# A graph-convolution lookup: ranks that count down, scans beside the roots, and the embedding product scaled one batch later

## The reference, cut to what matters

```python
def gcn_conv(x, W, b, row, col, num_nodes):
    h = x @ W
    loop = jnp.arange(num_nodes)
    row_sl = jnp.concatenate([row, loop]); col_sl = jnp.concatenate([col, loop])
    deg = jax.ops.segment_sum(jnp.ones_like(col_sl, dtype=h.dtype), col_sl, num_segments=num_nodes)
    dinv = jax.lax.rsqrt(jnp.maximum(deg, 1.0))
    norm = dinv[row_sl] * dinv[col_sl]
    return jax.ops.segment_sum(h[row_sl] * norm[:, None], col_sl, num_segments=num_nodes) + b

h1 = gcn_conv(emb, W1, b1, row, col, 25000)      # emb is 25000 x 64, W1 is 64 x 128
lookup = gcn_conv(h1, W2, b2, row, col, 25000)   # W2 is 128 x 64
return lookup[input]                             # 512 x 200 rows of 64
```

## Time and profile before

| | before |
|---|---|
| median of 3 runs | 6868.01 us |
| the profiled execution: its own time | 6869.0 us |
| the profiled execution: span of the profile | 6867.3 us |
| PE busy / DVE busy / ACT busy / POOL busy | 5034.4 / 4014.0 / 2327.5 / 4539.2 us |
| first gather, last gather of round 2, last lookup gather (start) | 786.6, 5835.4, 6857.8 us |
| mean granted TensorE clock | 0.672 |

### The profile page before, as it was taken

How to read it: one execution, slowest core, us unless ns; L and a number is a source line. 1 busy time by engine, 2 the same in 40 slices (tenths; PEclk the granted TensorE clock), 3 DMA queues, 4 the chain that set the end, 5 groups by cost and what they waited for, 6 DMA issues and landing times.

```text
span 6867.3 us, 134775 instructions
## 1 busy us (share of the span) xinstructions
PE 5034.4 (73%) x27534; PEld 4382.0 (64%) x27535; DVE 4014.0 (58%) x13643; ACT 2327.5 (34%) x6633; POOL 4539.2 (66%) x4736
## 2 busy tenths in 40 slices
PE   6868898998999999888788888888888888000000
PEld 5634476776776777888788888888888888000000
DVE  8977798788788798566566555555555555000000
ACT  7957798688688688211000000000000011000000
POOL 0000377777777777777677777777777777677777
PEclk9989999899899899555555555555555555555555
DMA  0001111111111111111111111111111111111111
GB/s 14 0 17 40 28 24 25 26 25 25 26 25 25 27 25 25 30 39 39 33 26 26 26 26 26 26 26 26 27 26 26 35 39 39 44 53 53 53 53 52
DMA packets 184478, 210.98 MB, mean 31 GB/s; under 512 B 81356, under 2 KB 100182, under 8 KB 184336
## 3 DMA queue, kind: packets, MB, share of 16 engines
q0 software_dynamic: 151040, 154.97, 11.4%
q1 hardware_dynamic: 15280, 35.45, 1.4%
q10 hardware_dynamic: 18016, 19.05, 1.0%
HBM read 163.62 MB, written 45.54 MB: 30 GB/s over the span
## 4 chain that ended last, share of the span: by engine, by line
PE 36%; POOL 30%; issue 17%; DVE 7%; DMA 7%; DVEq 2%; ACT 0%; POOLq 0%; SPq 0%; ACTq 0%
PE ps L667 25%; POOL scratch L381 19%; POOL acc L414 11%; PE ps L571 10%; DMA scratch<-table,source 7%; DVE hi_onehot L840 2%; DVE acc L1046 1%; DVE place_i L1001 1%; DVE late L1025 1%; PE ps L720 1%; DVE late L1036 1%; DVE scratch L840 0%; DVEq L1044 0%; DVEq L854 0%; DVE prt_onehot L840 0%
## 5 line engine op out<-in xcount | busy, mean ns | idle before, releaser
L381 POOL DMA_INDIRECT scratch<-table,source x3920 | 3780.5, 964 | 2051.2 <-issue 1104.7
L667 PEld LDWEIGHTS ps<-scratch,late 128*128 128x128 f32 x19520 | 3751.6, 286 | 822.4 <-issue 657.5
L667 PE MATMUL ps<-scratch,late 128*128 x19520 | 3738.9, 369 | 574.5 <-SPq L340 341.7
L1046 DVE TENSOR_TENSOR acc<-acc,ps 128x128 f32 x4880 | 1358.2, 278 | 1378.6 <-PE ps L667 1345.0
L1036 DVE TENSOR_SCALAR late<-ramp,target 128x256 f32<-128x256 f16 x4148 | 1564.2, 377 | 149.0 <-issue 71.5
L467 ACT ACTIVATE late<-prt_onehot,scratch 125x128 f16<-125x128 f16 x4000 | 1236.4, 387 | 306.3 <-DVE prt_onehot L840 151.2
L571 PE MATMUL ps<-late 125*128 125x488 f16 x4000 | 1128.3, 375 | 35.8 <-DVE late L1025 32.9
L414 POOL DMA_INDIRECT acc<-lookup,scratch x800 | 755.1, 944 | 267.4 <-issue 243.4
L543 ACT ACTIVATE acc<-acc,dinv (+1 forms) x196 | 57.5, 340 | 2441.5 <-DVE acc L1046 2441.5
L1025 DVE TENSOR_SCALAR late<-ramp,tcol 125x488 f16<-125x488 f16 x2000 | 697.6, 358 | 48.9 <-PE ps L571 48.3
L571 PEld LDWEIGHTS ps<-late 125*128 125x128 f16 x4000 | 397.6, 119 | 146.2 <-DVE late L1025 60.8
(11 more groups left out here) (149 smaller groups left out, 1106.6 us busy)
## 6 DMA issues: line engine op xcount, KB each, us to landing
scratch<-table,source POOLq DMA_INDIRECT x3920, 2.5
out<-acc SPq DMA_DIRECT2D x40, 640.0 KB, 3.0
acc<-lookup,scratch POOLq DMA_INDIRECT x800, 2.4
table<-acc SPq DMA_DIRECT2D x49, 128.0 KB, 2.5
table<-acc ACTq DMA_DIRECT2D x49, 128.0 KB
lookup<-acc ACTq DMA_DIRECT2D x49, 128.0 KB
late<-embT ACTq DMA_DIRECT2D x47, 128.0 KB, 2.7
scratch<-edge_index SPq DMA_DIRECT2D x2, 976.6 KB
```

The source lines that it names most:

```text
L381: pool.indirect_dma_start(out=place, out_offset=None, in_=table[r], in_offset=bass.IndirectOffsetOnAxis(ap=source[:, t:t + 1], axis=0)).th ...
L667: last = pe.matmul(visit_ps[odd * W8 + k][:, n * FEAT:(n + 1) * FEAT], target_onehot[:, odd * W8 + k, n * P:(n + 1) * P], row, start=True, ...
L1046: dve.tensor_tensor(dst, dst, visit_ps[odd * W8 + k].rearrange("p (n f) -> p n f", f=FEAT), ALU.add).then_inc(visits_added, 1)
```

## The change

There are six edits.

- **Ranks count down.** The three triangles hold -1 in place of 1 (three more memsets on GpSimd). A slot's ranks start at its end and fall. The running sum of the counts, which ends each slot, is used as it comes out of the scan, so that the reduction per block and the subtraction of the counts are gone. Whether a block is empty is now found by comparing neighbouring block ends.
- **Seeds are shifted as they are copied.** The shift of each block's seeds to its first tile was one operation over all 3920 seeds. Now a small array `shift` (5 x 98) is made, and each `seed_ranks` applies it while it writes to PSUM.
- **Scans run beside the roots.** The five scans over the slots stand right after `deg`, each waiting only for its own chunk's counts, ahead of the wait for the square root.
- **The embedding product is scaled a batch later.** VectorE scales the product of batch s-1 in batch s, right behind the block one-hots.
- **Its matmuls are spread.** The eight passes of L720 stand in pairs between the column placements 2 to 5.
- **SyncE loads `embT`.** The load leaves ScalarE's queue and stands in `write_first`, ahead of the wait for the scaled group.

Besides, `w1_sb`, `w2_sb` and `b1_rep` share memory with a one-hot buffer that is idle at the start.

The diff, cut to its core:

```diff
@@ SyncE
                 for s in range(GROUPS):
+                    if s + 2 < GROUPS:
+                        sp.wait_ge(emb_multiplied, s + 1)
+                        sp.dma_start(emb_sb[:, s % 2, :], embT[:, (s + 2) * EN:(s + 3) * EN]).then_inc(emb_loaded[s % 2], 16)
                     sp.wait_ge(emb_scaled, s + 3)
                     sp.dma_start(table_v[0][:, s * ET:(s + 1) * ET, :], acc[:, s * ET:(s + 1) * ET, :]).then_inc(first_written, 16)
@@ GpSimd
+            for triangle in (before, after, itself):
+                pool.memset(triangle[:, :], -1.0).then_inc(ints_made, 1)
+            pool.wait_ge(ints_made, 10)
-            pool.affine_select(out=before[:, :], in_=ones[:, :], compare_op=ALU.is_gt, fill=0.0,
+            pool.affine_select(out=before[:, :], in_=before[:, :], compare_op=ALU.is_gt, fill=0.0,
...
@@ ScalarE, sort_batch
                 for j in range(W8):
                     scale_column(s, j, b)
-                    if load and j == W8 - 2:
-                        act.wait_ge(emb_multiplied, s + 1)
-                        act.dma_start(emb_sb[:, b, :], embT[:, bass.ds((s + 2) * EN, EN)]).then_inc(emb_loaded[b], 16)
@@ TensorE, sort_batch
                 rank_rest(s + 1)
-                pe.wait_ge(emb_loaded[b], i * 16 + 16)
-                pe.wait_ge(emb_scaled, s + 1)
-                for k in range(ET):
+                for j in range(2, W8):
+                    place_column(s, j)
+                    if j >= 2 + ET:
+                        continue
+                    if j == 2:
+                        pe.wait_ge(emb_loaded[b], i * 16 + 16)
+                        pe.wait_ge(emb_scaled, s + 1)
+                    k = j - 2
                     last = pe.matmul(emb_ps[b][:, k * FEAT:(k + 1) * FEAT], emb_sb[:, b, k * P:(k + 1) * P], w12[:, :],
                                      start=True, stop=True)
-                last.then_inc(emb_multiplied, 1)
-                for j in range(2, W8):
-                    place_column(s, j)
+                    if k == ET - 1:
+                        last.then_inc(emb_multiplied, 1)
@@ VectorE, from the degrees on
             dve.wait_ge(turned_degrees, 1)
-            step(dve.tensor_scalar(deg..., 1.0, 1.0, ALU.add, ALU.max))
+            root(dve.tensor_scalar(deg..., 1.0, 1.0, ALU.add, ALU.max))
+            step = chain(base_step)
+            dve.wait_ge(ramps_cast, 2)
+            for c in range(CHUNKS):
+                dve.wait_ge(counts_summed, c + 1)
+                step(dve.tensor_tensor_scan(seed[:, c, :], counts[:, c * SLOTS:(c + 1) * SLOTS], zeros_f[:, 0:SLOTS],
+                                            0.0, ALU.add, ALU.add))
             dve.wait_ge(root_taken, 1)
...
-            step(dve.tensor_reduce(flat, per_slot, AX.X, ALU.add))
-            for c in range(CHUNKS):
-                step(dve.tensor_tensor_scan(seed[:, c, :], counts[:, c * SLOTS:(c + 1) * SLOTS], zeros_f[:, 0:SLOTS],
-                                            0.0, ALU.add, ALU.add))
...
-            step(dve.tensor_tensor(seed_flat, seed_flat, counts[:, :], ALU.subtract))
-            step(dve.tensor_tensor(flat_i, seed_slot[:, :, 0], flat, ALU.add))
+            block_end = seed[:, :, :].rearrange("p c (n j) -> p c n j", j=W8)[:, :, :, W8 - 1]
+            step(dve.tensor_copy(tot_i, block_end))
             step(dve.tensor_scalar(low_i, flat_i, P - 1, None, ALU.bitwise_and))
             step(dve.tensor_scalar(flat_i, flat_i, 7, None, ALU.logical_shift_right))
-            step(dve.tensor_scalar(flat, flat, 0.0, None, ALU.is_gt))
+            step(dve.tensor_scalar(tot[:, :, 0:1], block_end[:, :, 0:1], 0.0, None, ALU.is_gt))
+            step(dve.tensor_tensor(tot[:, :, 1:NB], block_end[:, :, 1:NB], block_end[:, :, 0:NB - 1], ALU.is_gt))
             step(dve.scalar_tensor_tensor(flat, low_i, 0.0, flat, ALU.is_gt, ALU.mult))
...
-            step(dve.tensor_tensor(low_flat, end_flat, flat, ALU.subtract))
-            step(dve.scalar_tensor_tensor(seed_slot, low_flat.unsqueeze(2).broadcast_to([P, CHUNKS * NB, W8]), float(P),
-                                          seed_slot, ALU.mult, ALU.add))
+            step(dve.scalar_tensor_tensor(shift[:, :, :].rearrange("p c n -> p (c n)"), end_flat, -1.0 / P, flat, ALU.add, ALU.subtract))
@@ VectorE, seed_ranks
                 for h in range(2):
-                    dve.tensor_copy(rank_ps[:, h, :].rearrange("p (j n) -> p j n", n=NB),
-                                    seed[:, c, :].rearrange("p (n j) -> p j n", j=W8)[:, h * W8 // 2:(h + 1) * W8 // 2, :]
-                                    ).then_inc(rank_seeded, 1)
+                    half = slice(h * W8 // 2, (h + 1) * W8 // 2)
+                    dve.scalar_tensor_tensor(rank_ps[:, h, :].rearrange("p (j n) -> p j n", n=NB),
+                                             shift[:, c, :].unsqueeze(1).broadcast_to([P, W8 // 2, NB]), float(P),
+                                             seed[:, c, :].rearrange("p (n j) -> p j n", j=W8)[:, half, :],
+                                             ALU.mult, ALU.add).then_inc(rank_seeded, 1)
@@ VectorE, sort_batch
                 block_onehots(s + 1)
+                if emb:
+                    dve.wait_ge(emb_multiplied, s)
+                    dve.tensor_tensor(acc[:, bass.ds((s - 1) * ET, ET), :], emb_ps[1 - b]..., dinv[:, bass.ds((s - 1) * ET, ET)]...,
+                                      ALU.mult).then_inc(emb_scaled, 1)
                 column_onehot(s, 0, b)
...
                 cast_places(s + 1)
-                if emb:
-                    dve.wait_ge(emb_multiplied, s + 1)
-                    dve.tensor_tensor(acc[:, bass.ds(s * ET, ET), :], emb_ps[b]..., dinv[:, bass.ds(s * ET, ET)]...,
-                                      ALU.mult).then_inc(emb_scaled, 1)
                 partition_onehots(s + 1, 1 - b)
```

More of the change, by code:

```diff
@@ L146, in build @@
         seed = sb("seed", [P, CHUNKS, SLOTS], F32)
+        shift = sb("shift", [P, CHUNKS, NB], F32)
         DW = max(CV, CHUNKS * NB)
@@ L176, in build @@
         target = sb("target", [P, CHUNKS * CV], F32)
+        w1_sb, w2_sb, b1_rep = (lo_onehot[:, 0, :, :].rearrange("p j m -> p (j m)").bitcast(F32)[:, a:b]
+                                for a, b in ((0, FEAT), (FEAT, 2 * FEAT), (2 * FEAT, 2 * FEAT + P)))
         visit_source = lo_onehot[:, 0, :, :].rearrange("p j m -> p (j m)")[:, 0:2 * CV].bitcast(F32)
@@ L365, in _ @@
             pool.iota(visit_no_i[:, :], pattern=[[1, VP]], base=0, channel_multiplier=VP).then_inc(ints_made, 1)
-            pool.wait_ge(ints_made, 7)
-            pool.affine_select(out=before[:, :], in_=ones[:, :], compare_op=ALU.is_gt, fill=0.0,
+            for triangle in (before, after, itself):
+                pool.memset(triangle[:, :], -1.0).then_inc(ints_made, 1)
+            pool.wait_ge(ints_made, 10)
+            pool.affine_select(out=before[:, :], in_=before[:, :], compare_op=ALU.is_gt, fill=0.0,
                                base=0, pattern=[[1, P]], channel_multiplier=-1).then_inc(triangles_made, 1)
-            pool.affine_select(out=after[:, :], in_=ones[:, :], compare_op=ALU.is_gt, fill=0.0,
+            pool.affine_select(out=after[:, :], in_=after[:, :], compare_op=ALU.is_gt, fill=0.0,
                                base=0, pattern=[[-1, P]], channel_multiplier=1).then_inc(triangles_made, 1)
-            pool.affine_select(out=itself[:, :], in_=ones[:, :], compare_op=ALU.is_equal, fill=0.0,
+            pool.affine_select(out=itself[:, :], in_=itself[:, :], compare_op=ALU.is_equal, fill=0.0,
                                base=0, pattern=[[1, P]], channel_multiplier=-1).then_inc(triangles_made, 1)
@@ L479, in act_onehot, with sort_batch @@
                                scale=-1.0).then_inc(act_onehots, 1)
-            def sort_batch(i, k, load):
+            def sort_batch(i, k):
                 s, b = i * STEPS + k, k % 2
@@ L486, in sort_batch @@
                     scale_column(s, j, b)
-                    if load and j == W8 - 2:
-                        act.wait_ge(emb_multiplied, s + 1)
-                        act.dma_start(emb_sb[:, b, :], embT[:, bass.ds((s + 2) * EN, EN)]).then_inc(emb_loaded[b], 16)
             for s in range(STEPS):
-                sort_batch(0, s, True)
-            with act.Fori(1, LOOPED) as i:
+                sort_batch(0, s)
+            with act.Fori(1, LOOPED + 1) as i:
                 for k in range(STEPS):
-                    sort_batch(i, k, True)
-            for s in range(LOOPED * STEPS, CB):
-                sort_batch(*divmod(s, STEPS), s + 2 < GROUPS)
+                    sort_batch(i, k)
+            for s in range((LOOPED + 1) * STEPS, CB):
+                sort_batch(*divmod(s, STEPS))
             def columns(s, b, between=None, odd=0):
@@ L875, in _ @@
                                   counted[:, c, :].unsqueeze(1).broadcast_to([HIGH, NB, W8]), ALU.mult).then_inc(counts_spread, 1)
-            step = chain(deg_step)
```

(16 more changed lines are left out.)

22 lines of the change are left out of this document (6 added, 16 removed).

## The result

The changed kernel takes 6849.57 us (median; 6845.27 to 6854.5) against 6868.01 before, a ratio of 0.9973 with a 95% interval from 0.9963 to 0.9982. It is faster by 18 us, where 64 were forecast; the range began at 6793 and ended at 6832. The bases came out as predicted, and the batches gave next to nothing. The two profiled executions took 6869.0 us before and 6854.5 after, so their spans differ by 14.5 us and not by the 18 of the medians.

What follows compares the result with a forecast made beforehand. Preparation before the first gather, then GpSimd's back-to-back gathers, were taken to bound the kernel. Bases 19.4 us plus batches 45.1 us gave 64.5 us off 6869.0, forecast 6804 us, range 6793 to 6832 us.

Steps and rivals of the forecast that it cites:

- The bases: VectorE's chain of bases before the batches of chunk 0: edits there save 19.4 us, between 18 and 20.
- the batches: Chunk 0's 49 batches carrying the product: period falls from 6.62 to 5.70 us, saving 45.1 us.
- What bounds the kernel: Preparation until GpSimd's first gather at 786.6 us, then 6081 us at fixed distance; preparation savings shorten the end one for one.
- the strided copy (L915): In the bases, L915 becomes a copy of the same 490 strided elements, priced the same: 1.07 us with its gap.
- the move of the scans: In the bases, five scans of 9.1 us move into VectorE's idle time before the root: worth 7.4 us.
- the price of a pair: TensorE's pair of product passes: 0.26 us from the run, or 0.20 where it takes turns with columns.
- The scaling a batch later: VectorE's 0.42 us multiply is covered by its 0.56 us wait for `rank_before`, with about 0.2 us margin.
- the prediction's period: One batch of chunk 0, minimum to minimum: 5.54 us at best, 5.78 at worst, 5.70 taken.
- no wait of L1131's multiply above 0.5 us: Sign expected in the profile after: VectorE's multiply of the product never waits longer than 0.5 us.
- The product stays serial: Rival: passes cost their full 1.03 us on the loop or the multiply comes too late; 6827 us, chance 0.17.
- The batches give nothing: Rival: another wait of the same size takes its place, only the bases count; 6849 us, chance 0.04.
- The load: Rival: `embT`, queued on SyncE behind table writes, starves TensorE; 6919 us at 15 us a load, chance 0.03.

Runs made afterwards that it cites:

- The stacked kernel: Changed kernel with two embT tiles stacked in 128 rows, w12 twice on the diagonal, two matmuls behind columns 2 and 3, two load DMAs: 6779.36 us.
- e9_act_load: Changed kernel with embT loaded by ScalarE's queue between columns 6 and 7, as before the change: 43.9 us slower than the kernel before, ratio 1.0062.
- e3_serial: Changed kernel with the product's eight passes in one run ahead of column 2, still 64 rows: 54.7 us faster than the kernel before, ratio 0.9924.
- e11_serial_in_place: Changed kernel with the passes in one run (64 rows), scaled in their own batch, embT loaded by SyncE: 17.2 us faster than before, ratio 0.9974.

## Why the prediction was wrong

- **What bounds the kernel** held: the time moved with the first gather in every run. The stacked kernel's first gather is 91.1 us earlier (695.5 against 786.6) and its time 89.0 us shorter; that of e9_act_load is 40.5 us later and its time 43.9 longer.
- **The bases** held: 19.7 us of 19.4. Two terms of it were off by some tenths and nearly cancelled: the strided copy (L915) took 0.60 us, not 1.04, and the move of the scans paid 9.1 - 2.0 = 7.1 of 7.4 us, 2.0 being the later start of the reciprocal (390.76 against 388.77). The comparison of two strided streams (L920) took 1.03 us and the seeds 0.82 apiece, as taken.
- **The step that failed** is the price of a pair: "A pair of passes costs 0.26 (1.03 / 4), or 0.20 where it takes turns with columns". Both rows were read for the wrong thing. Rows 5 has the product's own rows, but in one run, where the change of rows is paid once; rows 9 has the alternation, but of matmuls with 128 rows. The pair with 64 rows between columns measured 0.47, outside both bounds, and four of them made 1.88 us where 1.04 were allowed at most. With 65 or 128 rows it measured 0.17, below both bounds. The rest of the working stands: with p for a pair, the prediction's period is 5.14 + 2p + (2p - 0.4), and with 0.47 that is 6.62, measured 6.58. The form of L720, 64*128, was in rows 5, and the trace before had a gap of 0.09 us in front of the run (the product starts 0.43 us after the last `rank_rest` row, a column, in the profile after, 0.34 after that row); I took neither for a price.
- **The scaling a batch later** held: covered, 37 us in the one-run kernels (e3_serial against e11_serial_in_place). The sign "no wait of L1131's multiply above 0.5 us" failed (1.15 to 1.44 us), but the margin of VectorE stayed just positive, so this is not what set the period.
- **The rivals.** "The product stays serial" had the right place, pairs that cost their full price on the loop, but priced the four at 1.03 us where they took 1.88; it left 22 us to be gained and set the upper end of the range, which is why the result lies outside. "The batches give nothing", at 6849 us with a chance of 0.04, has the measured number by coincidence: no other wait of the same size took over. The scaling a batch later gave 37 us, and the spreading took 36 back (e3_serial against the changed kernel).
- **The load** was no rival to fear on SyncE: between 446 and 740 us TensorE never waited for it. I had not seen that it was needed: left on ScalarE's queue, it would have made the change slower by 62 us.

## What to carry to other kernels

Price an instruction that is moved by a row in which it has its new neighbours and its own shape; where no row has both, the range must hold what the missing one could cost. Here each visit of TensorE to a matmul over 64 rows between matmuls over 125 cost about 0.3 us more than the same over 65 or 128, however many passes it had. So pad such a matmul or, better, stack two in the 128 rows, before spreading it. And a wait that stands in the order of an engine with spare time is harmless only as long as what it waits for stays early: moving the producer later needs the wait moved too.

## What the runs showed of the hardware that was not expected

- 64 contracted rows against 65: a pair of fp32 passes of 64 columns between fp16 columns takes 0.47 against 0.17 us, at a granted clock of 1.00 (the 2.4 GHz level) in both traces. A run of four such pairs is dearer by the same 0.3 us.
- A VectorE copy of 490 fp32 elements at a stride of 8 with a cast to int32 took 0.60 us, while an addition with one such stream took 1.04 and a comparison with two of them 1.03: here two strided streams cost no more than one, and a copy with one cost less than either.
